# A four-layer graph network on one core: early gathered columns and an early projection in set-up, one more batch of made columns in the last edge stage, and an in-place row expansion in PSUM

## The reference

```python
# layer 0 (attention over edges)
xl, xr = x @ W_l + b_l, x @ W_r + b_r
g = leaky_relu(xl[src] + xr[dst] + edge_attr_16 @ W_e, 0.2)
logits = einsum('ehc,hc->eh', g, att)              # softmax over the edges of a node
out = segment_sum(xl[src] * alpha, dst) + bias      # then batch norm, gelu
# layer 1: q = x @ Wq; weights wk, wv = relu(edge_attr_64 @ w1 + b1) @ w2 + b2 ; softmax over edges
# layer 2: score = exp(clip(sum(k[src] * q[dst]) / 8, -5, 5)); weighted sum of v[src] / (sum + 1)
# layer 3 (64 relations): rel[n, r] = x[n] @ W[r];  h = segment_sum(rel[src, etype] * norm, dst)
```

## Time and profile before

| | us |
|---|---|
| median of 3 runs (5065.47 to 5067.86) | 5067.24 |
| the profiled execution | 5067.32 |
| its span, first to last instruction | 5065.2 |
| set-up and first projection, until the first gather of `edges_0` | 128.1 |
| gathers of `edges_0`, first to last start | 128.1 to 1115.5 |
| gathers of `edges_2` | 3059.7 to 3891.6 |
| gathers of `edges_3` | 4125.9 to 4983.6 |

### The profile page before, as it was taken

The page is one execution under the profiler, slowest core; times in us unless marked ns, Lnnn a source line. Parts: engine busy times, 40 slices in busy tenths (PEclk is TensorE's granted clock), DMA queues, the critical chain, the costliest instruction groups (busy, mean ns, idle before and its releaser), DMA issues. The chain is left out here.

```text
span 5065.2 us, 56169 instructions
## 1 busy us (share of the span) xinstructions
PE 3897.9 (77%) x16729; PEld 2708.3 (53%) x16729; DVE 4002.1 (79%) x5626; ACT 2086.4 (41%) x3715; POOL 3706.0 (73%) x3427
## 2 busy tenths in 40 slices
PE   1788888872999999999999956888883666666651
PEld 0455555542888888888888843333331442233321
DVE  3888888874899999999999856999996656767653
ACT  0666676661344444444444423545453322222221
POOL 4777777764788888888888637777776567777774
PEclk8999999995999999999999957999996778888875
DMA  7777777763788888888888643444443662222221
GB/s 294 270 274 274 267 274 269 274 221 120 292 316 321 324 316 325 318 317 326 316 319 325 240 93 112 130 129 131 130 127 98 239 246 65 68 69 66 69 58 45
DMA packets 354911, 1072.41 MB, mean 212 GB/s; under 512 B 96662, under 2 KB 119762, under 8 KB 310292
## 3 DMA queue, kind: packets, MB, share of 16 engines
q1 hardware_dynamic: 237364, 854.18, 44.8%
q0 software_dynamic: 103232, 158.19, 12.3%
q10 hardware_dynamic: 14112, 57.81, 2.8%
HBM read 677.38 MB, written 392.57 MB: 211 GB/s over the span
## 5 line engine op out<-in xcount | busy, mean ns | idle before, releaser
L1742 PE MATMUL COLS<-CF,XF 128*128 128x256 f32 x6272 | 1485.9, 380 | 6.2 <-DVE XF L1850 6.2
L1742 PEld LDWEIGHTS COLS<-CF,XF 128*128 128x128 f32 x6272 | 1135.0, 190 | 130.4 <-DVE XF L1850 6.6
L1018 ACT ACTIVATE OUT<-SC 128x576 f32<-128x576 f32 (+3 forms) x392 | 577.9, 1474 | 1083.7 <-DVE SC L953 727.3
L1709 POOL DMA_INDIRECT G<-x_tab,SRC x784 | 834.4, 1064 | 230.0 <-issue 218.1
L901 POOL DMA_INDIRECT G<-xl_tab,SRC x784 | 749.7, 956 | 239.0 <-issue 238.7
L901 POOL DMA_INDIRECT G<-rel_tab,REL x680 | 651.7, 958 | 210.1 <-issue 206.9
L901 POOL DMA_INDIRECT G<-kv_tab,SRC x640 | 638.1, 997 | 195.1 <-issue 194.8
L1323 PE MATMUL PICK<-HOT,KV 125*128 125x512 bf16 x2700 | 628.8, 397 | 141.1 <-ACT TURNED L1355 123.8
L1491 PE MATMUL MADE<-XM,W 128*128 128x512 f32 x832 | 460.5, 710 | 198.7 <-DVE XM L1579 198.6
L1323 PEld LDWEIGHTS PICK<-HOT,KV 125*128 125x128 bf16 x2700 | 272.2, 101 | 490.8 <-issue 185.3
L1850 DVE TENSOR_TENSOR XF<-XT,SHB 128x4096 f32<-128x4096 f32 x98 | 432.5, 4413 | 0.0
(11 more groups left out here) (296 smaller groups left out, 6977.5 us busy)
## 6 DMA issues: line engine op xcount, KB each, us to landing
SHB<-ea9t SPq DMA_DIRECT2D x196, 1024.0 KB
wkv_tab<-WKV SPq DMA_DIRECT2D x98, 1024.0 KB, 6.2
WKV<-wkv_tab SPq DMA_DIRECT2D x98, 1024.0 KB, 5.9
scan<-OUT SPq DMA_DIRECT2D x196, 288.0 KB, 4.7
scan<-OUT ACTq DMA_DIRECT2D x98, 576.0 KB
rel_tab<-YS SPq DMA_DIRECT2D x50, 1024.0 KB
RAW<-spread SPq DMA_DIRECT2D x196, 256.0 KB
spread_q<-ZQ SPq DMA_DIRECT2D x98, 512.0 KB, 4.0
```

The lines of the kernel that those rows point to most:

```text
L1018: nc.scalar.activation(self.OUT[d][:, :, 0:WD], SC[b][:, 0:WD, 1:1 + C].rearrange("p r j -> p j r"), ACT.Copy).then_inc(self.copied_out, 1)
L1709: pool.indirect_dma_start(out=e.G[0][b][:, col, :], out_offset=None, in_=x1_tab, in_offset=bass.IndirectOffsetOnAxis(ap=SRC[:, at:at + 1], ...
L1742: nc.tensor.matmul(acc, XF[b][:, k, edges_], CF[:, k, :], start=(k == 0), stop=False)
```

## The change

It has six parts.

1. Set-up takes over the first projection. The transposes of `X`, the products, `TAB`, the stores of both tables and the scatter move into the set-up block, and the phase and its barrier go. The first three zero pieces are issued by ACT.
2. 32 columns of layer 0 (`EARLY`; the last column of chunks 2, 5, ..., 95) are gathered from `x` itself in set-up, 4 before the segment gathers and 28 behind them, with a `drain` of POOL after. PE transposes and projects them, DVE adds the bias, and they stay in SBUF as `XEARLY`. `edges_0` gathers 752 columns; SP places each early column in its buffer by a transfer of 32 KB.
3. `spare_products` is gone, and `hide` stands ahead of `project_attributes`.
4. `edges_2` expands in place: `XE` is `XI`, in PSUM.
5. In `project_relations` the doubled copies `XX` move from POOL to DVE, and the loads of `REL` and `EW_IN` move here from `edges_3`.
6. `BATCHES3` is 14: 112 made columns, 672 gathered.

```diff
+EARLY = 32
+EARLY_T = [2 + 3 * i for i in range(EARLY)]
+EARLY_FIRST = 4
+ROWS0_AT = [sum(C - (q in EARLY_T) for q in range(t % 4, t + 1, 4)) for t in range(NCH)]
-BATCHES3 = 13
+BATCHES3 = 14
...
@@ set-up, SP
+                    sp.dma_start(SRC_EARLY[:, :], src_early).then_inc(src_early_in, 16)
...
-                    blank_spread(range(3))
...
+                    sp.wait_ge(rows_made, 7)
+                    for i, tab in enumerate((xl_tab, xr_tab)):
+                        sp.dma_start(tab.rearrange("(p k) f -> p k f", k=K), TAB[:, :, 64 * i:64 * i + 64])\
+                          .then_inc(tables_out, 16)
+                    sp.wait_ge(tables_out, 32)
+                    sp.wait_ge(spread_zeroed, 16 * BLANKS)
...
@@ set-up, POOL
+                    pool.wait_ge(src_early_in, 16)
+                    gather_early(0, EARLY_FIRST)
                     for part, (k0, k1) in enumerate(PARTS):
                         pool.wait_ge(seg_known, min(part, len(SEARCH) - 1) + 1)
...
+                    gather_early(EARLY_FIRST, EARLY)
+                    pool.drain()
+                    pool.wait_ge(starts_known, 1)
+                    pool.wait_ge(rows_made, 7)
+                    pool.wait_ge(spread_zeroed, 16 * BLANKS)
+                    for k in range(K):
+                        pool.indirect_dma_start(
+                            out=spread, in_=TAB[:, k, 64:128], in_offset=None,
...
@@ set-up, ACT
+                    act.wait_ge(zeroed, 1)
+                    blank_spread(act, range(3))
...
@@ project_relations, POOL
-                        for k0, m in GROUPS[1:]:
-                            nc.gpsimd.tensor_copy(XX[:, k0:k0 + m, 0, :], X[:, k0:k0 + m, :]).then_inc(doubled, 1)
-                            nc.gpsimd.tensor_copy(XX[:, k0:k0 + m, 1, :], X[:, k0:k0 + m, :]).then_inc(doubled, 1)
...
@@ project_relations, DVE
+                        double(1)
                         split(0)
...
+                            if g == 7 and k in DOUBLE_AT:
+                                double(DOUBLE_AT[k])
...
@@ Edges, layer 2
                         self.XI = [self.wide("XI", 64)] * 2
-                        self.XE = [sb("XE", [P, 64, 1 + C], F32, ctx)] * 2
+                        self.XE = self.XI
...
@@ edges_0, SP
+                        def place_early(t):
+                            i = EARLY_T.index(t)
+                            wait(sp, e.weighted, t - 3)
+                            sp.dma_start(e.G[0][t % 4][:, C - 1, :], XEARLY[:, i, :]).then_inc(early_in[i % 2], 16)
...
@@ edges_0, POOL
-                            e.gather(pool, t, C, SRC, e.weighted)
+                            e.gather(pool, t, C - (t in EARLY_T), SRC, e.weighted)
...
@@ edges_0, PE
-                                spare_products()
+                                hide(t + 1, n + b, 1 - b, False)
                                 project_attributes(t + 1, n + b, 1 - b, False)
-                                hide(t + 1, n + b, 1 - b, False)
```

More of the change, by code:

```diff
@@ L273, in graph_kernel, with blank_spread @@
             tposed, t_copied = s("tposed"), s("t_copied")
+            def blank_spread(eng, pieces):
+                for a in pieces:
+                    eng.dma_start(spread.rearrange("(p a m) f -> p a (m f)", a=BLANKS, m=56)[:, a, :]
+                                  .rearrange("p (r f) -> p r f", r=4),
+                                  ZERO[:, :].unsqueeze(1).to_broadcast([P, 4, 14 * 64]))\
+                       .then_inc(spread_zeroed, 16)
             with nc.Block() as block:
@@ L288, in _ @@
                     sp.dma_start(WO_T[:, :], wout).then_inc(loaded, 16)
[L289 to L296, removed]
-                    blank_spread(range(3))
+                    sp.dma_start(W_EARLY[:, :], w_early).then_inc(w_early_in, 16)
                     sp.wait_ge(ridx_ready, 1)
@@ new lines, in _ @@
+                    for u, (k0, m) in enumerate(GROUPS):
+                        pe.wait_ge(x_copied, u + 1)
+                        if u >= 2:
+                            pe.wait_ge(rows_made, u - 1)
+                        for c in range(m):
+                            last = nc.tensor.matmul(PO[u % 2][:, c * P:(c + 1) * P],
+                                                    XT[:, (k0 + c) * P:(k0 + c + 1) * P], wcol("W_l", "W_r"),
+                                                    start=True, stop=True)
+                        last.then_inc(rows_done, 1)
@@ new lines, in _ @@
+                    pe.wait_ge(w_early_in, 16)
+                    pe.wait_ge(x_early_in, 16 * EARLY)
+                    for i in range(EARLY // 8):
+                        if i >= 1:
+                            pe.wait_ge(early_copied, i)
+                        for q in range(4):
+                            c = 8 * i + 2 * q
+                            last = nc.tensor.transpose(PE_T[:, q * P:(q + 1) * P],
+                                                       XEARLY[:, c:c + 2, :].rearrange("p c f -> p (c f)"),
+                                                       IDENT[:, :])
+                        last.then_inc(early_turned, 1)
+                        pe.wait_ge(early_copied, i + 1)
+                        if i >= 1:
+                            pe.wait_ge(early_made, i)
+                        for q in range(4):
+                            last = nc.tensor.matmul(PE_W[:, q * P:(q + 1) * P], XET[:, q * P:(q + 1) * P],
+                                                    W_EARLY[:, :], start=True, stop=True)
+                        last.then_inc(early_done, 1)
@@ L1149, in project_attributes @@
                               .then_inc(projected, 1)
-                        def spare_products():
-                            for a in range(2):
-                                nc.tensor.matmul(HID[:, 512 * a:512 * a + 512], IDENT[:, :],
-                                                 WE8[:, :, :].rearrange("p j f -> p (j f)"), start=True, stop=True)
                         def step(t, n, b, first, last):
@@ L2431 @@
     w2[0:64, 0:128], w2[64:128, 128:256] = a["L1_gnn_k_w2"], a["L1_gnn_v_w2"]
+    src_cols = padded(a["src"].astype(np.int32), EPAD).reshape(P, J)
+    w_early = np.zeros((P, P), f32)
+    w_early[0:64, 0:64] = w_early[64:128, 64:128] = a["L0_gnn_W_l"]
     arrays = {
@@ L2458 @@
         "basis": a["L3_gnn_basis"],
+        "src_early": np.stack([src_cols[:, t * C + C - 1] for t in EARLY_T], axis=1),
+        "w_early": w_early,
     }
```

116 lines of the change are left out of this document (90 added, 26 removed).

## The result

| | before | changed |
|---|---|---|
| median of 6 runs each, us | 5066.97 | 5024.55 (5022.12 to 5028.54) |
| ratio, 95% interval | | 0.9914 (0.9904 to 0.9923) |
| span of the profiled execution | 5065.2 | 5023.8 |

The account below looks back on a forecast made before the run. POOL's gather issue was taken to bound the edge stages of layers 0, 2 and 3. Terms -40.4 + 1 + 3 - 0.4 + 1.6 - 3.2 - 10.1 = -48.5 from 5067.3 gave 5019 us, range 5008 to 5048.

Parts of the forecast that it names:

- The limit of the first stage: First edge stage: POOL's gather issue stays the limit at 9.68 us a chunk, above DVE's 8.95 and the PE/ACT loop's 7.92.
- The first rival: First edge stage stays at its present loop, about 9.95 us a chunk, gaining 13 instead of 39; 5045 us, chance 0.13.
- 32 x 1.261: First edge stage: 32 gathers fewer at 1.261 us each, -40.4 us.
- The clock: PE in the first edge stage: without spare products the clock sometimes falls, share between 0.8 and 1.0; +1 us.
- The third rival: PE's clock in the first edge stage falls more than once a step, 1.48 us a fall; 5136 us, chance 0.09.
- the `drain` falls in the same slack ... at most what would carry it past 92.6: Set-up: POOL's drain after the early gathers hides before the zeros land at 92.6; at least 0, at most 6 us.
- The second rival: Set-up is ended by POOL's early gathers at 1.8 us each, scatter 11 later instead of 3; 5027 us, chance 0.12.
- POOL's pace sets this stage too, so the gain shows only in its last chunk: Third stage: faster DVE scores save about 0.4 us a chunk, but only the last chunk shows it; -0.4 us.
- still ahead of DVE's last instruction: Relation phase: 8 more gathers end near 4116, before DVE's last instruction at 4120.26 + 0.99, so POOL does not end it.
- the stores' +1.6: Relation phase: stores of `rel_tab` fill the DMA queues, so 8 more gathers cost 0.195 us each, +1.6 us.
- REL's wait: Moving the index loads into the relation phase removes POOL's 3.17 us wait for REL; -3.2 us.
- The fourth rival: Batch 14 gains nothing: made columns come late or the relation phase grows by the stage's loss; 5029 us, chance 0.06.

Follow-up runs that it names:

- e8: Changed kernel with the first edge stage's leaky step reading its second input from PSUM instead of SBUF; 5012.75 us, against the changed kernel's 5024.55.
- e5: Changed kernel with PE's two spare products of the first edge stage back and HID after PROJ; 5043.42 us, against the changed kernel's 5024.55.
- e6: Kernel before the change with the spare products taken out and HID ahead of PROJ, nothing else; 5077.79 us, ratio 1.0021 to the kernel before.
- e2: Changed kernel without POOL's drain in set-up; 5970.63 us on a chip where the kernel before takes 5939.09.
- e7: Changed kernel with 16 early columns instead of 32; 5041.55 us, against the changed kernel's 5024.55.
- e3: Changed kernel with XE of the third edge stage in SBUF again; 5891.59 us on a chip where the kernel before takes 5939.09.
- e11: Changed kernel with XE of the third edge stage in SBUF again, on another chip; 5959.81 us, against the changed kernel's 5997.81 there.
- e4: Changed kernel with 13 made batches instead of 14; 5946.64 us on a chip where the kernel before takes 5939.09.
- e10: Changed kernel with 13 made batches instead of 14, on another chip; 5984.19 us, against the changed kernel's 5997.81 there.

## Why the prediction came out right, and where its steps did not

- **The limit of the first stage** was read rightly: POOL, at its issue. e8 shows the pace without losses (1.249), and that PE's and ACT's loop is under 9.57 a chunk. The loop before, read as 9.94 from one step, was 9.91 in e5. The first rival fails with that.
- **"32 x 1.261"** was mis-sized by what I had taken as a constant. The 1.261 holds 8.0 us of lengthened gathers; the changed stage has 17.6. That more of them are lengthened took 9.3 of the forecast 40.4 away, where I had put down 1, for the clock. e8 shows it: without them the stage takes 938.0.
- **The clock**: 0.94 as forecast (0.8 to 1.0), price zero in e8, and e6's 8.3 us are accounted for without it. The third rival wanted more than 1.5 falls a step; there are 30 in 98 steps, 33 in e8 and 34 in e6, against 2 with spare products (before, e5). I had reckoned with one a chunk. The rule of the Trainium skill that the prediction cites against the removal (TensorE: Matmul & The Clock Gate, "HAM oscillation — how this bites in real kernels") has a fall in every round; the trace agrees that falls come without the products and not that every round has one, and its case, matmul bursts shorter than the waits, is not this loop's, where PE is busy 718.93 of 956 us. Removing the spare products alone does make the kernel slower (e6), for another reason, and is worth 14.9 us once POOL is faster (e5).
- **Set-up**: the step that failed is "the `drain` falls in the same slack ... at most what would carry it past 92.6". It was passed 8.1 us behind the last gather's start, at 98.4, against zeros that had landed at 93.1. The zeros moved by 4.3 where I had +3; the other 5.3 is POOL, whose last early gather also started at 90.27, where I had 87. Taking the drain out did not bring the 5.3 back (e2), keeping it ahead of the zeros did (e7). The second rival named the place, and its price (11 later) was nearer than my 3, but by gathers of 1.8 us, while they came every 1.31.
- **Third stage**: "POOL's pace sets this stage too, so the gain shows only in its last chunk" is wrong, by 9.2 us. The pace itself held 18.1 us from this very step, by the rows of this chip; the runs that put XE back (e3, e11) show the lengthened gathers but went the other way in time, on chips where POOL is not the limit. The row for it was there: gathers of 1.302 us where others had 1.26, and a maximum of 1847 ns.
- **Relation phase**: "still ahead of DVE's last instruction" compared the gather's end, not the drain that stands behind it. That drain costs 4.2 us; the stores' +1.6 did not come (SP 149.7 us behind the first store before, 149.9 now). REL's wait gave 2.6 of 3.2. The phase came out 3.3 us longer than forecast. The fourth rival, that batch 14 gains nothing, did not come: the last stage is 12.7 us shorter and the phase, with the drain in it, 1.7 longer. What batch 14 alone is worth, e4 and e10 do not show.
- **Last stage**: 1.7 of the 2.6 us beyond the forecast are again long gathers (9.2 us before, 7.5 now); the other 0.9 is not accounted for.

The misses are +8.3 in the first stage, +6.6 in set-up and +3.3 in the relation phase on one side, -9.2 and -2.6 on the other. The total was within 6 us of the forecast mostly because they cancel, which is luck.

## What to carry to other kernels

Where POOL issues gathers as the pace of a stage, look at the spread of one gather's duration, not its mean, and match the long ones with what DVE does at their start; a DVE step with two SBUF inputs, a bf16 mask or a fill is paid by POOL, and moving one input to PSUM is worth more there than on DVE (18.3 us of the first stage in e8, with DVE's step no shorter). Give the moved tile a buffer of its own where there is room: in place it cost 52 us on a chip where POOL was not the limit. A change on any other engine that shifts the phase between the two changes this loss, up or down. When POOL's last transfer of a phase moves, count the drain behind it, and read a stage's end at the next phase's first instruction, not at the last gather.

## What the runs showed of the hardware

- A gather that starts more than 0.04 us into a DVE step with two SBUF inputs, and more than 0.15 ahead of its end, ends 0.81 us behind that step (1.45 us instead of 0.94 at worst in a step of 0.70; 1.85 in one of 1.08). A gather that started ahead of the step does not hold it (at most 0.72 us, 64 times). With one input in PSUM: 0.94, in 0 of 752 longer than 0.983.
- A fill of 128x360 f32 in SBUF, 0.36 us long, holds gathers too (1.80 us with the step behind it).
- POOL's drain is passed 11.2 to 11.7 us behind the start of the last of 104 or 112 gathers, 8.1 behind that of the early ones, and 4.4 behind the last of 25 scatters that follow a drain; without that drain it is 9.1 behind them. In set-up the last packet of the gathers accounts for 5.3 of the 8.1; what else it waits for no row shows.
- On two of the three chips of the experiments the same kernel takes 17 to 19% longer, with the same durations of single gathers, ACT copies and DVE steps. On one of the two the change that gains 0.86% in the first measurement gains 0.34%.
